# Routing of each batch moved into the attention's next turn, in a token, text-encoder, attention and mixture-of-experts kernel

## What is computed

```python
h = concatenate([layernorm(patches @ W_proj.T + b_proj) * gamma + beta,   # 49 rows of a batch
                 text_encoder(emb[x_txt] + pe)], axis=1)                  # 512 rows, 4 layers
# attention, 12 heads of 64
qkv = layernorm(h) @ W_qkv.T
dots = einsum('bhid,bhjd->bhij', q, k) * scale
dots = where(diag, MASK_VAL, dots)
h = h + (softmax(dots) @ v) @ W_out.T + b_out       # called "fused" in the kernel
# experts, 2 of 8
x = layernorm(h)                                    # no gain, no offset
probs = softmax(x @ gate_w)
top_w, top_i = top_k(probs, 2)
y_e = gelu(x @ w_up[e] + b_up[e]) @ w_down[e] + b_down[e]
h = h + sum over the two experts of top_w * y_e
```

## Time and profile before

| | us |
|---|---|
| median of 3 runs | 4368.94 (4368.18 to 4373.55) |
| the profiled execution's own time | 4374.97 |
| its span, first to last instruction | 4373.2 |
| encoder, from 0 to | 2281.4 |
| attention, 2281.4 to | 3689.1 |
| route, 3689.1 to | 3811.3 |
| place, 3811.3 to | 3943.3 |
| blocks, to the end | 4373.2 |

### The profile page before, as it was taken

The page is one execution under the profiler, slowest core; times in us unless marked ns, Lnnn a source line. Parts: engine busy times, 40 slices in busy tenths (PEclk is TensorE's granted clock), DMA queues, the critical chain, the costliest instruction groups (busy, mean ns, idle before and its releaser), DMA issues. The chain is left out here.

```text
span 4373.2 us, 64449 instructions
## 1 busy us (share of the span) xinstructions
PE 3810.5 (87%) x21850; PEld 2532.1 (58%) x21850; DVE 2232.9 (51%) x3419; ACT 2119.3 (48%) x3230; POOL 1101.8 (25%) x1004
## 2 busy tenths in 40 slices
PE   4899999999999999999856999999999996408998
PEld 2455555555555555555534677666766774307887
DVE  6566666666666666666524444444444442213443
ACT  0554554554555545545414766755756663003332
POOL 5132332322332322323210000000000001063444
PEclk7899999999999999999977999999999998558999
DMA  7333233242343342333114111111111112335664
GB/s 174 93 101 105 87 106 102 87 117 87 90 119 93 94 117 79 101 108 92 48 48 116 31 34 27 31 35 23 35 31 24 37 28 96 103 112 161 148 145 107
DMA packets 265492, 368.62 MB, mean 84 GB/s; under 512 B 49616, under 2 KB 166400, under 8 KB 261824
## 3 DMA queue, kind: packets, MB, share of 16 engines
q1 hardware_dynamic: 232752, 285.52, 23.1%
q0 software_dynamic: 22960, 57.40, 5.8%
q10 hardware_dynamic: 9600, 23.26, 1.6%
HBM read 235.77 MB, written 116.32 MB: 81 GB/s over the span
## 5 line engine op out<-in xcount | busy, mean ns | idle before, releaser
L641 DVE TENSOR_REDUCE mx<-ring 128x2 f32<-128x1024 f32 x768 | 920.0, 1223 | 505.8 <-PE ring L404 502.8
L533 ACT ACTIVATE probs<-ring 128x1024 f32<-128x1024 f32 x768 | 767.2, 1024 | 418.0 <-PE ring L417 417.0
L1430 DVE TENSOR_REDUCE a_nmx<-a_ring 128x1 f32<-128x561 f32 (+1 forms) x480 | 341.6, 737 | 309.1 <-PE a_ring L1271 158.9
L1320 ACT ACTIVATE a_ring<-a_ring,a_nmx 128x561 f32<-128x561 f32 (+1 forms) x480 | 333.8, 695 | 197.8 <-DVE a_nmx L1430 194.8
L404 PE MATMUL ring<-k_stack,q_stack 48*128 48x512 f32 x1536 | 360.0, 481 | 63.5 <-ACT probs L533 23.1
L417 PE MATMUL ring<-q_stack,k_stack 64*128 64x512 f32 x1536 | 363.5, 490 | 51.9 <-DVE mx L641 39.2
L431 PE MATMUL acc<-probs,vals 128*32 128x512 f32 x3072 | 400.6, 642 | 1.3 <-ACT probs L533 1.3
L1201 POOL TENSOR_SCALAR_AFFINE_SELECT a_probs<-a_probs 128x256 f32<-128x256 f32 (+1 forms) x240 | 91.9, 383 | 1227.4 <-ACT a_probs L1352 1227.4
L1352 ACT ACTIVATE a_probs<-a_ring 128x561 f32<-128x561 f32 (+1 forms) x480 | 287.4, 637 | 169.2 <-PE a_ring L1268 166.4
L1268 PE MATMUL a_ring<-a_k_hh,a_q_hl 128*128 128x256 f32 (+1 forms) x960 | 311.1, 339 | 22.6 <-DVE a_q_hl L1410 11.0
L417 PEld LDWEIGHTS ring<-q_stack,k_stack 64*128 64x128 f32 x1536 | 142.6, 189 | 285.9 <-DVE mx L641 102.0
(11 more groups left out here) (220 smaller groups left out, 6801.8 us busy)
## 6 DMA issues: line engine op xcount, KB each, us to landing
q_stack<-qk_scratch SPq DMA_DIRECT2D x576, 64.0 KB, 2.3
k_stack<-qk_scratch SPq DMA_DIRECT2D x576, 64.0 KB, 2.4
qk_scratch<-qk_hi SPq DMA_DIRECT2D x32, 768.0 KB, 3.6
qk_scratch<-qk_lo SPq DMA_DIRECT2D x32, 768.0 KB, 5.1
a_q_hm<-a_q_hl SPq DMA_DIRECT2D x48, 280.5 KB
a_k_hh<-a_k_hh SPq DMA_DIRECT2D x48, 280.5 KB
tokens<-h_out SPq DMA_DIRECT2D x33, 384.0 KB, 2.5
h_in<-tokens SPq DMA_DIRECT2D x32, 384.0 KB, 4.3
```

Of the source, the lines that this page charges most:

```text
L533: nc.scalar.activation(probs[n % 2][:, pair:pair + 2, x // 2, :], buf[:, :, :], ACT.Exp, scale=DK ** -0.5).then_inc(act, 1)
L641: nc.vector.tensor_reduce(mx[s][:, i, :].rearrange("p (r t) -> p r t", r=2)[:, :, t], buf[:, :, :], AX, ALU.max).then_inc(dve, 1)
L1320: nc.scalar.activation(buf, buf, ACT.Exp, bias=nmx[0:r, i, h:h + 1], accum_out=sums[0:r, i, h:h + 1]).then_inc(act, 1)
L1430: nc.vector.tensor_reduce(nmx[0:r, i, h:h + 1], flat(buf)[0:r, 0:N], AX, ALU.max, negate=True).then_inc(dve, 1)
```

## The change

`route_phase` and `place_phase` are gone. Their work is a new stream `r` of 80 letters in `A_ORDER` (`ROUTE`), done per batch of 5 tiles, one batch behind the attention: turns 2 to 8 route batches 1 to 7, and the last batch's runs behind the last output projection in `A_CLOSE`.

- Norm: from `a_tok` in SBUF, not read back from `fused`. `r_xw` (5 tiles of 208) is what is scattered.
- Gate: no transposes and no product on PE; DVE multiplies each row with 4 experts' weights (`mult`, 128x4x192) and sums (`add`), ten times each for a batch.
- Selection and places: as before but on 5 tiles. PE's two counting products are one more job of the ring (`count`).
- Blocks are given out as they fill: an expert keeps a current block over the batches and takes the next free number when it is full. The rows carry the weights of all eight experts; `blocks_phase` picks its own by `mine` (one more small product and one sum per block in place of a copy).
- Scatter: 10 indirect DMAs per batch on POOL in the turn.
- The output projection has 4 steps rather than 5 (the last two tiles share one buffer).
- The attention's beginning: the first rows are loaded first, weights that are not needed at once have an own semaphore; of four clearing instructions of 6744 columns on DVE or of 2 partitions by as many, DVE keeps one and POOL gets one. POOL sets up the route's tables behind the first norm.
- The table's seven DMAs are issued by SP in the encoder's last turn, and the 25 empty blocks are filled by SP between that turn and the encoder's rest; DVE makes the empty rows there.

```diff
@@ attention order @@
+ROUTE = ([("r", x) for x in ("stats", "rsqrt", "norm")] + [("r", x, j) for j in range(10) for x in ("mult", "add")]
+         + [("r", x) for x in ("top", "less", "exp", "total", "inv", "share", "gt", "eq", "tie", "over", "rank", "mark", "is_k", "sel")]
+         + [("count",)] + [("r", "weight")] + [("r", "run", i) for i, _ in TILES]
+         + [("r", x) for x in ("pos", "new1", "new2", "cum", "ends", "past", "first", "taken", "offset", "delta", "high", "high_by",
+                               "in_cur", "in_new", "pick", "slot_f", "slot", "rest", "cur1", "cur2", "cur3", "cur4", "own1", "own2",
+                               "own3", "own4")]
+         + [("scatter", i, k) for i, _ in TILES for k in range(2)])
-        "w": [("wo", i) for i, _ in TILES],
+        "w": [("wo", i) for i in range(4)],
...
+        "r": ROUTE}
...
-A_FIRST = batch_steps(["w"])
+A_FIRST = batch_steps(["w", "r"])
-A_CLOSE = [("wo", i) for i, _ in TILES]
+A_CLOSE = [("wo", i) for i in range(4)] + ROUTE
@@ DVE, the new steps @@
+                if what == "stats":
+                    await_step(v, R, it, "dve", ("wo", 3), now)
+                    for i, r in TILES:
+                        ins = nc.vector.bn_stats(stats2[0:r, i, :], tok[0:r, i, :])
...
+                elif what == "norm":
+                    v.wait_ge(rst2, per_batch(R, it, 2, 0))
...
+                    for i, r in TILES:
+                        ts(xw[0:r, i, 0:D], tok[0:r, i, :], mv2[0:r, i, 0:1], rstd2[0:r, i:i + 1], ALU.subtract, ALU.mult)
+                elif what == "mult":
+                    j = step[2]
+                    after(*(("add", j - 1) if j else ("norm",)))
+                    row = xw[:, j // 2:j // 2 + 1, 0:D].to_broadcast([P, 4, D])
+                    ins = tt(prod[:, :, :], row, gate[:, 4 * (j % 2):4 * (j % 2) + 4, :], ALU.mult)
+                elif what == "add":
+                    j = step[2]
+                    after("mult", j)
+                    ins = add_up(logits[:, j // 2, 4 * (j % 2):4 * (j % 2) + 4], prod[:, :, :], AX, ALU.add)
...
@@ PE and POOL @@
+                    elif kind == "count":
+                        pe.sem_inc(tick, 1)
+                        await_step(pe, R, it, "route", ("r", "sel"), now)
+                        for k, t in enumerate((before, ones)):
+                            last = nc.tensor.matmul(buf[:, k, 0:5 * E], t[:, :], sel[:, :, :].rearrange("p i e -> p (i e)"),
+                                                    start=True, stop=True)
...
+                    elif step[0] == "scatter":
+                        i, k = step[1:]
...
+                        g.indirect_dma_start(slots_in, bass.IndirectOffsetOnAxis(ap=slot[0:r, k, i:i + 1], axis=0),
+                                             xw[0:r, i, :], None).then_inc(scattered, 16)
@@ attention's beginning @@
+            nc.gpsimd.memset(q_hm[:, :, :].bitcast(F32), 0.0).then_inc(ready, 1)
...
-            for t in (q_hm, k_l1):
-                nc.vector.memset(t[:, :, :].bitcast(F32), 0.0).then_inc(ready, 1)
...
-            nc.vector.memset(k_l1[DH:DH + 2, :, :].bitcast(F32), 1.0).then_inc(ready, 1)
...
+            nc.vector.memset(k_l1[:, :, :].bitcast(F32), 1.0).then_inc(ready, 1)
@@ encoder's end, SP @@
             steps(R_FINAL, 0)
+            sp.wait_ge(blank, 2)
+            for n in range(NBLOCKS):
+                sp.dma_start(slots_in[n * BLOCK:(n + 1) * BLOCK, :].rearrange("(p i) d -> p i d", i=4), empty).then_inc(filled, 16)
...
             store(R_CLOSE, 0, 0, 6, 0)
```

More of the change, by code:

```diff
@@ L1086, in attention_phase @@
         half = sb("a_half", [P, 5])
+        E = EXPERTS
+        gate = sb("r_gate", [P, E, D])
+        lane = sb("r_lane", [P, 1])
+        invalid = sb("r_invalid", [P, 1])
+        before = sb("r_before", [P, P])
+        ones = sb("r_ones", [P, P])
+        upto = sb("r_upto", [P, E, E])
+        numbers = sb("r_numbers", [P, NBLOCKS])
+        xw = sb("r_xw", [P, 5, XW])
+        stats2 = sb("r_stats", [P, 5, 6])
+        mv2 = sb("r_mv", [P, 5, 2])
+        rstd2 = sb("r_rstd", [P, 5])
@@ new lines, in attention_phase @@
+        var_eps2 = sb("r_var_eps", [P, 5])
+        prod = sb("r_prod", [P, 4, D])
+        in_prod = prod[:, :, :].rearrange("p e d -> p (e d)")
+        gate_raw = vals[:, 0:2, :, :].rearrange("p i h d -> p (i h d)")
+        logits = sb("r_logits", [P, 5, E])
+        top = sb("r_top", [P, 5])
+        pr = sb("r_pr", [P, 5, E])
+        total = sb("r_total", [P, 5])
+        over, same = (in_prod[:, 5 * E * E * k:5 * E * E * (k + 1)].rearrange("p (i e f) -> p i e f", e=E, f=E) for k in range(2))
@@ new lines, in attention_phase @@
+        past = in_prod[:, 0:NBLOCKS * E].rearrange("p (n e) -> p n e", e=E)
+        cum = in_prod[:, 10 * E * E:11 * E * E].rearrange("p (e f) -> p e f", f=E)
+        rank = sb("r_rank", [P, 5, E])
+        is_k = sb("r_is_k", [P, 2, 5, E])
+        sel = sb("r_sel", [P, 5, E])
+        count = sb("r_count", [P, 2, 5, E])
+        part = sb("r_part", [P, 2, 5, E])
+        run = sb("r_run", [P, 6, E])
+        place = sb("r_place", [P, 5, E])
+        high = sb("r_high", [P, 5, E])
+        one, new, ends, first, offset, delta, current, begin = (sb(f"r_{n}", [P, E]) for n in (
+            "one", "new", "ends", "first", "offset", "delta", "current", "begin"))
@@ L1151, in steps @@
                             sp.wait_ge(stored, per_batch(R, it, 32, BASE))
+                            sp.sem_inc(tick, 1)
+                            await_step(sp, R, it, "route", ("r", "norm"), now)
                         sp.sem_inc(tick, 1)
@@ L1212, in _ @@
                 steps(R_LOOP, it)
-            steps(R_FINAL, 0)
+            for R in (R_FINAL, R_CLOSE):
+                steps(R, 0)
+            g.wait_ge(scattered, 160 * B)
         @block.tensor
@@ L1326, in steps @@
                         nc.scalar.activation(logs[:, :, :], sums[:, :, GH * g:GH * g + GH], ACT.Ln).then_inc(act, 1)
+                        continue
+                    if step == ("r", "exp"):
+                        await_step(sc, R, it, "route", ("r", "less"), now)
+                        nc.scalar.activation(pr[:, :, :], logits[:, :, :], ACT.Exp).then_inc(act, 1)
                         continue
@@ L1388, in steps, with name_blocks @@
+            def name_blocks():
+                v.wait_ge(route, R_CLOSE.end()["route"])
+                ts(which[:, :], owner[:, :], float(P), lane[:, 0:1], ALU.mult, ALU.add)
+                tt(mine[:, :, :], owner[:, :].rearrange("p (n a) -> p n a", a=1).to_broadcast([P, NBLOCKS, E]),
+                   numbers[:, 0:E].rearrange("p (a e) -> p a e", a=1).to_broadcast([P, NBLOCKS, E]), ALU.is_equal).then_inc(route, 1)
             def steps(R, it):
@@ L1390, in steps @@
                     kind = step[0]
-                    if kind == "ln":
+                    if kind == "r" and step[1] not in ("rsqrt", "exp"):
+                        route_step(R, it, step, now)
+                    elif kind == "ln":
                         (moments, normalise)[step[1]](R, it)
@@ L1460, in _ @@
                 steps(R, 0)
+            name_blocks()
 T_ALL = (B * N + P - 1) // P
[L1464 to L1465 removed]
 BLOCK = 4 * P
```

602 lines of the change are left out of this document (282 added, 320 removed).

## The result

The changed kernel takes **4202.03 us** (median of 4 runs, 4201.37 to 4204.3) beside 4368.56 (4 runs, 4364.14 to 4373.55): ratio 0.9621, 95% interval 0.9606 to 0.9636, faster. The forecast was 4197, its range 4152 to 4264.

What follows compares the result with a forecast made beforehand. PE was taken to bound attention and blocks, with 257.7 us of almost idle PE between. Terms -201 - 24.5 + 52.5 + 1 = -172 from 4374.97 gave 4203, median forecast 4197 us; range 4152 to 4264.

Steps and rivals of the forecast that it cites:

- Tail, 201: Between last output addition and the blocks: 257.7 us shrink to 56.4, only the last batch's routing exposed; 201 us saved.
- Beginning, 24.5: Attention's start: table DMAs off ACT and fewer DVE clearings let ACT copy sooner; 24.5 us saved, between 17 and 27.
- Turns, 7.5 each: Seven attention turns with routing beside PE: each 7.5 us longer, 52.5 in all.
- I take 6: Turn's stretch from head 6's maximum to next normalisation: 42.1 us of DVE work for 38, costing 6 us a turn.
- 1 us: The 125.8 us of a turn behind the crowded stretch: DVE goes from 53.9 to some 64, costing 1 us.
- PE's own 0.5: PE's additions in each routed turn: two products of 0.25 us each.
- Selections "at nothing": POOL in a turn: six scatters ahead of a diagonal selection cost nothing, since selections were waited for only once before.
- Encoder's end, 1, and the blocks, nothing: Encoder's end: five small DVE instructions on the path lose 1 us; blocks: two small DVE instructions per block cost nothing.
- All is hidden: Rival for the turns: idle DVE hides the routing, only 1.5 us a turn, 4155 us; chance 0.17.
- The clock falls: Rival for the turns: PE's short waits bring half clock, 18 us a turn, 4270 us; chance 0.17.
- POOL holds the selections back: Rival for the turns: slowed scatters ahead of selections make PE wait, 8 us a turn more, 4253 us; chance 0.08.
- Slower: Rival for the turns: routing isn't beside PE at all, each turn 36 us longer, 4397 us; chance 0.03.

Runs made afterwards that it cites:

- Both halves: Two runs against the changed kernel: table DMAs issued by ACT at the attention's start again, ratio 0.9681; DVE clearing three tiles as before, POOL none, 0.9656.
- e_spread_wide: Changed kernel with another order: gate instructions spread by DVE's idle time, selection, count and places later, scatters behind the last selection; 4182.31 us, ratio 0.9588.
- e_best: e_tuned_wide's order with small DVE instructions moved from right before the last transposed shift, and POOL's set-up behind the first normalisation; 4148.46 us, ratio 0.9511.
- e_scatters_last: Changed kernel with only the order altered: a turn's ten scatters all stand behind its last selection on POOL; 4186.07 us, ratio 0.9587.
- e_tuned_wide: Changed kernel with the 80 routing letters placed by a replay's search, gate never before steps without slack, scatters last; 4172.33 us, ratio 0.9573.
- e_pool_later: Changed kernel with POOL's set-up of the route's tables moved behind DVE's first normalisation; a single run, 4199.85 us.

## Why the prediction was right, and where it was not

- **Tail, 201:** 200.0. Each term came out within 0.4 but for the last, 1.4 more.
- **Beginning, 24.5:** 24.5 at PE's first projection of the first turn, by the chain that the prediction named. Both halves were tried, and neither alone gives it. POOL's clearing took 5.72 for 6.4. Not in the sum: 0.96 on DVE's normalisation.
- **Turns, 7.5 each:** 7.3 in the first routed turn, 7.0 on average. The size was right, in part by luck: 6 for the crowded stretch and 1 behind it were together 1.9 too much, and 1.65 stood at other places for which the sum had too little or nothing.
  - "I take 6" for the crowded stretch: 5.1, with DVE busy for 35.8 of 38.8 us, 92%. The stretch was read too long: from the place of the routed rows' normalisation to the next batch's it is 32.6 us before (2901.03 to 2933.59), with DVE busy for 16.6. The step that failed is the reason, that there is more work than time in it. The same work spread over twice the time cost nearly as much (e_spread_wide, 5.4 of the change's 7.3 in the turn), and the same work in the same turn at other places cost 0.5 (e_best), though its gate is spread as widely (53 to 141 us of the turn, for 50 to 136 in e_spread_wide). That rules out the amount of work in a stretch as the cause. What costs instead, a long instruction in front of a step whose buffer PE takes next without slack, is the rule by which the replay placed them; two orders bear it out in the first routed turn (0.4 and 0.5), but no run moves a single instruction.
  - "1 us" for the 125.8 us behind it: nothing but what the next two points name. DVE's added work was also put too high, 35.3 us a turn: its busy time goes from 77.55 to 105.6, 28 us more.
  - PE's own 0.5: 0.8 with the count's place in the ring.
  - Selections "at nothing": 1.25 a turn, 8.8 in all, taken away by e_scatters_last. Six scatters ahead of a selection were named and priced at nothing because the selections had been waited for once before; but two scatters in a row are 2.5 us, and the last selection had no such slack.
- **Encoder's end, 1, and the blocks, nothing:** the attention starts 0.2 later. The blocks are 1.5 longer; with the change they take 430.6 to 432.8 in the traces, all above the 429.9 of the one trace of before, so the added instructions may cost some 2 us there. That isn't shown.
- **Rivals.** *All is hidden* was not the change's outcome, but e_best shows that an order exists for which it holds. *The clock falls*: it did not. The crowded stretch ran at 1.00 with its waits of up to 1.2 us; the half-clock stretches (1.2 GHz) moved to the turn's start, and their sum over the seven routed turns is as before, 31 us in both traces. In e_tuned_wide PE ran at 0.51 from 2846 on, behind a wait of 1.8 us that ended at 2844.7, but its sum is 31 us too. The Trainium skill (TensorE: Matmul & The Clock Gate, "A second HAM failure mode") tells of a kernel that lost throughput because PE idled briefly but often; with the change's 41 waits for ACT in place of 27 the traces show no more of that than before. *POOL holds the selections back*: true in kind, 1.25 us a turn and not 8. Its 1.9 us for a scatter rested on the scatters that add into `fused`, another form; those of the routing took 0.97 in the middle and 1.16 at most. *Slower*: far off.

## What to carry to other kernels

Work put beside a full engine can cost by where it stands in the queue more than by its sum: lay the jobs of the full engine side by side, before and after, read off the few places that grow, and move the long instructions away from steps with no slack. A busy share doesn't tell: here one and the same 105 us of DVE work cost 7 us in the first routed turn in one order and half a microsecond in another. And when two engines must both be early for a third, find both chains; moving the later one alone gains only the difference between them, and moving the earlier one alone next to nothing.

## What the runs showed of the hardware

In the pairs seen here DVE and POOL hold each other up. The normalisation of five tiles took 1.53 us alone, 2.49 beside a POOL clearing of 0.96, and 4.90 beside that clearing and a copy of 2.74; with POOL behind it (e_pool_later) it is 1.53. A DVE subtraction of two SBUF operands of 8 columns took 1.92 beside POOL's addition of 2.35, at the same place in six turns. The Trainium skill (SBUF — State Buffer, "SBUF: two separate sides") says that DVE and POOL share a pair of ports, which one of them holds for a whole instruction while the other is blocked, where the DVE instruction is in a two-port mode, or has two SBUF inputs and the POOL instruction reads SBUF; the traces agree with it. The gate's products, which have two SBUF inputs, were never slowed (0.943 to 0.960), but one selection in each of the seven turns was: 1.174 to 1.178 us for 0.41, each with a gate product that began 0.04 us before it.

Also not expected: two transfers of 8.8 KB each, issued behind the first two of ten indirect scatters in a row, were followed by a wait of PE of 1.7 to 2.5 us, where the same ones issued ahead of the scatters were not. The trace has no time of their landing, and how much of this is the scatters' traffic was not tried apart.
